# The first rows of a fused convolution in another order, and its products in 64 slots instead of 72

## The chip, the cores and the metric

One core of one Trainium2 chip runs the whole program. The metric is the device time of one execution in microseconds (us), and lower is better.

## The reference, cut to what matters

Two layers are computed on x (8, 256, 512). The change lies in the first block alone, a gated causal convolution ("long convolution" with 32 filters, heads of 8 channels). In it k and v are both the context and q is the normalised x:

```python
k_ = k.reshape(B, H, head_dim, L)
...
kv = jnp.einsum('bhil,bhjl->bijhl', k_, v_)
...
y = jnp.fft.irfft(kv_f * kernel_f, n=fft_size)[..., :L]
out = y + kv * D[None, None, None, :, None]
out = jnp.einsum('bijhl,bhil->bjhl', out, q_)
...
x = x + jnp.tanh(g_xattn[0]) * _L0_xattn_ref(ctx_2048, ctx_2048, _layernorm(x, axis=-1), L0_xattn_ssm_kernel, L0_xattn_D, 8)
```

Here B is 8, H is 32, head_dim is 8 and L is 512. As k equals v, only 36 of the 64 products (i, j) of a head differ. All three later blocks (a mixture of experts, linear attention, soft mixture of experts) start from this block's output and are the same in both kernels.

## The kernel before

`conv_stage` is one block in which every engine has a program written out by hand. Only semaphores join them. What stands in an engine's program behind an instruction that waits, waits too.

**Rows.** The context rows (`c`) and the x rows (`q`) are turned by TensorE in units of 8 transposes of 128x128: `("c", 0, 0..3)` and `("q", 0, 0..3)` for the first half of the heads, `("c", 1, ..)` and `("q", 1, ..)` for the second. A unit fills one of three banks of the PSUM tensor `ring`. ScalarE (`put`) and, for the units named in `by_dve`, VectorE for one half of it, copy it to `c_e` or `q_e`. Before x rows are turned, VectorE takes their statistics (`normalise`), ScalarE the root (`ln.root`), and VectorE writes the normalised rows (`scale`). There are four such norms, of 4 row blocks each.

**Steps.** There are 16 steps of two heads. In step s VectorE makes the products of the context with itself for step s+2 (`pairs`, into `prod`), ScalarE rounds them to float16 (`split`, `prod_hi`), and GpSimd subtracts to get the rest (`prod_lo`, L299). TensorE multiplies both with Toeplitz tiles `toep`, read from a DRAM copy `ssm_split` of the filters that the kernel itself stores at the start: `convolve(s, m)` for m = 0 to 3, with 6(m+1) matmuls of 288 columns, 60 in a step. VectorE multiplies the result with q (`weigh(s, m)`, L429 to L431) into the slots of `terms`, 16 columns each. TensorE sums the slots by accumulating transposes (`add_up`, L524), 9 of them for 72 slots, 8 of which hold zeros from a memset. VectorE adds the residual (`add_rows`, L440). TensorE's order is `convolve(s, m)` and then the sum of two positions earlier; a `ring` bank is reused after three units and `terms` has three buffers. The turns of the second half stand between the positions of steps 1 to 4.

**Queues.** The SP queue loads rows and residuals and stores results. The ACT queue stores `ssm_split` and loads every `toep`. Behind that, GpSimd and ScalarE split the experts' down weights in 24 parts (`load_part`, `rest_of_parts`, `split_parts`), which the next stage needs. ScalarE's program in step s is: load `toep` for step s+1, its puts, `split(s + 2)`, `split_parts(s)`.

Of the kernel before, what the change touches and what calls it, by code (L numbers as in the profile page):

```python
# [14 lines left out]
ACT = mybir.ActivationFunctionType  # L15
ALU = mybir.AluOpType
# [3 lines left out]
B, N, D = 8, 256, 512  # L20
# [100 lines left out]
PAIRED = 2 * B * PAIRS  # L121
SLOTS_T = 9
RUN = 8 * SLOTS_T
WRAP = SSM_I + 4
# [17 lines left out]
def conv_stage(nc, k, x, ctx, ssm_reversed, ssm_d, g_xattn, g_ffn, ssm_split, x1, down, down_whole, down_tail):  # L142
# [5 lines left out]
    with phase(nc) as st:  # L148
# [16 lines left out]

        ident_zeroed, ident_ready, gates_loaded, gates_ready, zeroed = (
            sem(n) for n in ("ident_zeroed", "ident_ready", "gates_loaded", "gates_ready", "zeroed"))
        ssm_loaded, d_added, ssm_hi, ssm_lo, ssm_stored = (sem(n) for n in ("ssm_loaded", "d_added", "ssm_hi", "ssm_lo", "ssm_stored"))
# [25 lines left out]
        units = [(t, 0, n) for t in "cq" for n in range(4)]  # L194
        later = {1: ("c", 0), 2: ("c", 2), 3: ("q", 0), 4: ("q", 2)}
        for s in range(STEPS):
# [5 lines left out]
        turns = {unit: n for n, unit in enumerate(u for u in units if u[0] != "conv")}  # L202
        by_dve = {unit: n for n, unit in enumerate(u for u in units if u[0] == "c" and not u[1])}

# [33 lines left out]
        @block.sync  # L238
        def _(sp):
            def load(t, g, u):  # L240
                for e in range(2):
                    src = (c_t if t == "c" else x_t)[g, e, :, u * 4:u * 4 + 4, :]
                    sp.dma_start(rows[t][e * 64:e * 64 + 64, u * 4:u * 4 + 4, :], src).then_inc(loaded[t][u], 16)

            def load_res(s):
                if s >= 2:
                    sp.wait_ge(added, s - 1)
                sp.dma_start(res[:, s % 2, :], rows_at(x, s)).then_inc(res_loaded[s % 2], 16)

            def store(s):  # L250
                sp.wait_ge(added, s + 1)
                sp.dma_start(rows_at(x1, s), gated[:, s % 2, :]).then_inc(stored[s % 2], 16)

            for t in "cq":
                for u in range(2):
                    load(t, 0, u)
            load_res(0)
            load_res(1)
            for u in range(2):
                sp.wait_ge(turned["c"], 2 * u + 2)  # L260
                load("c", 1, u)
            for u in range(2):
                sp.wait_ge(normed, 4 * u + 4)
                load("q", 1, u)
            for s in range(STEPS):
                store(s)
                if s + 2 < STEPS:
                    load_res(s + 2)
            for u in range(2):
                sp.wait_ge(stored[u], STEPS // 2 * 16)  # L270

        @block.gpsimd
        def _(pool):
# [3 lines left out]
                                    base=0, pattern=[[-1, P]], channel_multiplier=1).then_inc(ident_ready, 1)  # L277
            nc.gpsimd.memset(terms[:, :, :, :], 0.0).then_inc(zeroed, 1)

# [14 lines left out]
            for s in range(STEPS):  # L294
                u = s % 2
                pool.wait_ge(hi_done, s + 1)
                if s >= 2:
                    pool.wait_ge(conv_done, (s - 1) * KD)
                nc.gpsimd.tensor_tensor(prod_lo[:, u].rearrange("p k e r -> p (k e r)"), prod[:, u, :],  # L299
                                        prod_hi[:, u].rearrange("p k e r -> p (k e r)"), ALU.subtract).then_inc(lo_done, 1)  # L300
                if s == 0:
                    for n in range(PART_BUFS):
                        load_part(n)
                if s >= 2:
                    rest_of_parts(s - 2)
# [6 lines left out]
        def _(act):  # L312
# [3 lines left out]
            act.dma_start(k.gates[:, 2:4], g_ffn.partition_broadcast(P)).then_inc(gates_loaded, 16)  # L316
            act.wait_ge(gates_loaded, 32)
            nc.scalar.activation(k.tanh_gates[:, :], k.gates[:, :], ACT.Tanh).then_inc(gates_ready, 1)
            act.wait_ge(d_added, 1)
            nc.scalar.activation(ssm_q[:, 0, :], ssm[:, :], ACT.Copy).then_inc(ssm_hi, 1)  # L320
            nc.scalar.preload_act_table(ACT.Sqrt)
            act.wait_ge(ssm_lo, 1)
            act.dma_start(ssm_split.rearrange("s e q d -> e s (q d)"), ssm_q[:, :, :].rearrange("h q d -> h (q d)")).then_inc(ssm_stored, 16)
            act.wait_ge(ssm_stored, 16)
            for s in range(T_BUFS):
                toeplitz(act, s)

# [22 lines left out]

            for n in range(4):
                put(("c", 0, n))
            split(0)
            for n in range(2):
                ln.root(nc, act, n)
                put(("q", 0, 2 * n))
                put(("q", 0, 2 * n + 1))
            split(1)
            for s in range(STEPS):
                if s >= 1 and s - 1 + T_BUFS < STEPS:  # L360
                    act.wait_ge(conv_done, s * KD)
                    toeplitz(act, s - 1 + T_BUFS)
                if s in (2, 3):
                    ln.root(nc, act, s)
                if s in later:
                    t, first = later[s]
                    put((t, 1, first))
                    put((t, 1, first + 1))
                if s + 2 < STEPS:
                    split(s + 2)  # L370
                split_parts(s)

        @block.vector
        def _(dve):
# [4 lines left out]

            for n in range(4):  # L380
                dve.wait_ge(turned["c"], n + 1)
                for dst, src in turned_in(("c", 0, n), 1):
                    last = nc.vector.tensor_copy(dst, src)
                last.then_inc(out_dve, 1)

            def pairs(s):
# [18 lines left out]
            def weigh(s, m):  # L405
# [5 lines left out]
                if n == 0:  # L411
                    dve.wait_ge(out_act, turns["q", 0, 3] + 1)
                    dve.wait_ge(zeroed, 1)
                if s == GSTEPS and m == 0:
# [15 lines left out]
                nc.vector.tensor_tensor(to(40, (8 * 2 * B, 3), (2, 64)), values(8, (64, 3), (1, 64)), weights(1, (B, 3), (1, 64)), ALU.mult)  # L430
                last = nc.vector.tensor_tensor(to(64, (4 * 2 * B, 2), (2, 32)), values(32, (0, 2), (1, 32)), weights(4, (32, 2), (1, 32)), ALU.mult)  # L431
                last.then_inc(weighed, 1)
# [28 lines left out]
            pairs(0)  # L461
            for n in range(2):
                normalise(n)
                scale(n)
            pairs(1)
            dve.wait_ge(gates_ready, 1)
            for s in range(STEPS):
                weigh(s, 0)
                if s in (2, 3):
                    normalise(s)  # L470
                weigh(s, 1)
                if s in (2, 3):
                    scale(s)
                weigh(s, 2)
# [1949 lines left out]
```

## Time and profile before

| | us |
|---|---|
| median of 3 runs | 1817.76 |
| lowest, highest | 1815.56, 1821.31 |
| the profiled execution | 1817.87 |
| its span in the profile | 1816.1 |

The profiled execution is 0.11 above the median; 1.8 us of it lie outside the span. All times below are from the span's start. Of the page, TensorE is busy 87% of the span, VectorE 60%, ScalarE 42%, GpSimd 29%. The convolution ends with its last `add_rows` at 264.48; the next stage begins to load after the last store, and everything after it depends on that store.

A row of a timeline gives start, duration, engine, line and operation, tiles written and read, shapes and count; in brackets is the idle time before it and what ended that. A row with a count spans several instructions. A row of windows gives for a stretch the busy time and count of each engine, then TensorE's granted clock (1.00 is 2.4 GHz, 0.50 is 1.2 GHz), the busy share of the DMA engines and their rate.

### The profile page before, as it was taken

How to read it: one execution, taken by the hardware profiler on the slowest of the kernel's cores; microseconds unless marked ns; L12 is line 12 of the kernel's file. 1: busy time of each engine (PE TensorE's matmuls, PEld its weight loads, DVE VectorE, ACT ScalarE, POOL GpSimd, SP SyncE). 2: the span in 40 equal slices, each digit the busy share in tenths (PEclk: the TensorE clock that was granted, in tenths of full speed). 3: DMA queues.
4: the chain of work that ended last, by engine and by line, in shares of the span. 5: the costliest groups of instructions: out<-in, count | busy, mean ns of one | idle time of the engine just before them, and what ended most of it. 6: DMA issues, size and time to landing. Idle time of an engine off the chain costs nothing. (4 is left out here: it accounts for less than half of the span.)

```text
span 1816.1 us, 27604 instructions
## 1 busy us (share of the span) xinstructions
PE 1583.9 (87%) x9596; PEld 925.9 (51%) x9596; DVE 1083.5 (60%) x2154; ACT 754.6 (42%) x1390; POOL 519.0 (29%) x428
## 2 busy tenths in 40 slices
PE   2879985999979999777898984979999999999997
PEld 1668872444446666434453542445555555555554
DVE  4778854543632223277676857566767767675664
ACT  2543213333412233144343431465565646565462
POOL 2347850434422344333434332101102020101101
PEclk6889997999989999978999997989999999999999
DMA  9435545433475665353515124651432505142341
GB/s 191 96 92 144 160 137 178 134 110 111 153 208 147 175 180 150 121 199 116 159 63 162 59 93 149 260 108 42 88 68 60 110 23 121 23 104 52 65 85 44
DMA packets 274042, 215.18 MB, mean 118 GB/s; under 512 B 184514, under 2 KB 222914, under 8 KB 272274
## 3 DMA queue, kind: packets, MB, share of 16 engines
q1 hardware_dynamic: 232640, 152.53, 31.9%
q10 hardware_dynamic: 32034, 31.10, 5.9%
q0 software_dynamic: 9264, 30.15, 5.5%
q8 instruction: 66, 1.08, 0.2%
q14 instruction: 38, 0.31, 0.1%
HBM read 120.33 MB, written 49.63 MB: 94 GB/s over the span
## 5 line engine op out<-in xcount | busy, mean ns | idle before, releaser
L2018 POOL TENSOR_TENSOR s_h_lo<-s_h,s_h_hi 128x512 f16<-128x512 f32 x32 | 36.9, 1154 | 554.2 <-DVE s_h_hi L2229 554.2
L1205 DVE TENSOR_TENSOR e_h<-e_up,e_silu 128x352 f32<-128x352 f32 x39 | 20.5, 525 | 149.8 <-ACT e_silu L1164 146.5
L511 PE MATMUL ring<-prod_hi,toep 128*128 128x288 f16 x320 | 94.7, 296 | 13.5 <-DVE terms L431 12.9
L299 POOL TENSOR_TENSOR prod_lo<-prod,prod_hi 128x2304 f16<-128x2304 f32 x16 | 73.3, 4584 | 107.2 <-ACT prod_hi L341 107.2
L2247 PE MATMUL s_ring<-w_mu,s_xt_hi 128*128 128x512 f16 x256 | 98.7, 386 | 4.2 <-DVE s_xt_lo L2150 3.9
L2249 PE MATMUL s_ring<-w_mu,s_xt_lo 128*128 128x512 f16 x256 | 98.5, 385 | 0.0
L2248 PE MATMUL s_ring<-w_mu,s_xt_hi 128*128 128x512 f16 x256 | 98.4, 384 | 0.0
L2247 PE MATMUL s_acc<-w_w,s_g_hi 128*128 128x512 f16 x256 | 97.1, 379 | 0.1
L2247 PE MATMUL s_ring<-w_w,s_xt_hi 128*128 128x512 f16 x256 | 97.0, 379 | 0.0
L2248 PE MATMUL s_ring<-w_w,s_xt_hi 128*128 128x512 f16 x256 | 97.0, 379 | 0.0
L2249 PE MATMUL s_ring<-w_w,s_xt_lo 128*128 128x512 f16 x256 | 97.0, 379 | 0.0
L2249 PE MATMUL s_acc<-w_w,s_g_lo 128*128 128x512 f16 x256 | 97.0, 379 | 0.0
L2248 PE MATMUL s_acc<-w_w,s_g_hi 128*128 128x512 f16 x256 | 97.0, 379 | 0.0
L2155 DVE TENSOR_REDUCE s_top<-s_lg 128x1 f32<-128x512 f32 x64 | 43.9, 686 | 88.6 <-ACT s_lg L2061 88.4
L513 PE MATMUL ring<-prod_hi,toep 128*128 128x288 f16 x320 | 94.5, 295 | 0.0
L512 PE MATMUL ring<-prod_lo,toep 128*128 128x288 f16 x320 | 94.5, 295 | 0.0
L1164 ACT ACTIVATE e_silu<-e_gate 128x352 f32<-128x352 f32 x39 | 18.1, 463 | 174.8 <-PE e_up L1107 174.8
L2067 ACT ACTIVATE s_dt<-s_ring,s_slot_low 128x256 f32<-128x256 f32 x128 | 59.4, 469 | 52.4 <-DVE s_dq L2177 52.2
L2232 DVE TENSOR_TENSOR s_g_lo<-s_ring,s_g_hi 128x512 f16<-128x512 f32 x64 | 43.6, 690 | 58.7 <-ACT s_g_hi L2098 58.7
L524 PE MATMUL rows_total<-ident,terms 128*128 128x128 f32 x576 | 73.7, 274 | 0.0
L1083 POOL DMA_INDIRECT e_rows<-normed_rows,slot_token x39 | 37.4, 958 | 124.8 <-DMA e_xt<-e_rows 122.8
L781 POOL TENSOR_TENSOR h_lo<-silu_h,h_hi 128x512 f16<-128x512 f32 (+1 forms) x24 | 30.8, 1283 | 146.5 <-ACT h_hi L746 146.5
(376 smaller groups left out, 4771.0 us busy)
## 6 DMA issues: line engine op xcount, KB each, us to landing
expert_rows<-e_y SPq DMA_DIRECT2D x39, 256.0 KB
toep<-ssm_split ACTq DMA_DIRECT2D x16, 512.0 KB
a_part_in<-in_L_ffn_W ACTq DMA_DIRECT2D x32, 256.0 KB
w_split<-a_part_q ACTq DMA_DIRECT2D x32, 256.0 KB, 2.5
w_w<-w_split SPq DMA_DIRECT2D x8, 1024.0 KB, 15.5
stage<-in_L_ffn_gate_w SPq DMA_DIRECT2D x8, 704.0 KB
stage<-in_L_ffn_up_w SPq DMA_DIRECT2D x8, 704.0 KB
c_rows<-in_ctx SPq DMA_DIRECT2D x8, 512.0 KB
```

The costliest lines, as they stand in the source:

```text
L299: nc.gpsimd.tensor_tensor(prod_lo[:, u].rearrange("p k e r -> p (k e r)"), prod[:, u, :], prod_hi[:, u].rearrange("p k e r -> p (k e r)"), ...
L511: nc.tensor.matmul(out, w_hi, hi, start=(n == 0), stop=False)
L512: nc.tensor.matmul(out, w_hi, lo, start=False, stop=False)
L513: last = nc.tensor.matmul(out, w_lo, hi, start=False, stop=(n == m))
L524: last = nc.tensor.matmul(out, terms[:, n % M_BUFS, o * 8:o * 8 + 8].rearrange("p j n -> p (j n)"), k.ident[:, :], is_transpose=True, star ...
L1083: nc.gpsimd.indirect_dma_start(rows[:, n % U, :], None, xn, bass.IndirectOffsetOnAxis(ap=k.slot_token[:, n:n + 1], axis=0)).then_inc(gathe ...
L2067: last_ = A(dt[:, n % 2, e, :], ring[:, bank, e * N:(e + 1) * N], ACT.Exp, bias=slot_low[:, n % 4, e:e + 1], accum_out=slot_sum[:, 2 * n + ...
L2155: V.tensor_reduce(top[:, t, j:j + 1], lg[:, t, j * D:(j + 1) * D], AX.X, ALU.max).then_inc(S["top_done"], 1)
L2232: V.tensor_tensor(g[1][:, n % G_BUFS, :], ring[:, bank, :], g[0][:, n % G_BUFS, :], ALU.subtract).then_inc(S["g_lo"], 1)
L2247: mm(out_, a[0], b_[0], start=first, stop=False)
L2248: mm(out_, a[0], b_[1], start=False, stop=False)
L2249: return mm(out_, a[1], b_[0], start=False, stop=last_)
```

## The change

- **Slots.** The products of a position go to 64 slots, all of which are written: four multiplies by VectorE (512, 384, 64 and 64 elements) instead of three (512, 384, 128), 8 transposes in a sum instead of 9. The memset of `terms` and its semaphore are gone.
- **Filters.** ScalarE rounds the filters first. The tanh of the gates, with the table load that follows, stands behind the first two context puts. The first two `toep` loads move from ACT's queue to SP's, behind the x rows and a wait for `ssm_stored`, ahead of the residuals and the second half's context rows.
- **First kernel half.** `prod_lo` of step 0 is made by VectorE between statistics and scaling of the first norm, not by GpSimd. The loads of the first three weight parts move with GpSimd's program from step 0 to step 1.
- **x rows.** VectorE copies one half of units `("q", 0, 2)` and `("q", 0, 3)`. The root of norm 1 stands behind the put of the first x unit.
- **Second half.** The x rows are turned in steps 4 and 6 instead of 3 and 4. Norm 2 has its statistics in step 2 and its scaling in step 3, norm 3 in steps 4 and 5; before, each had both in one step, 2 and 3.

```diff
-SLOTS_T = 9
+SLOTS_T = 8
...
-        later = {1: ("c", 0), 2: ("c", 2), 3: ("q", 0), 4: ("q", 2)}
+        later = {1: ("c", 0), 2: ("c", 2), 4: ("q", 0), 6: ("q", 2)}
...
-        by_dve = {unit: n for n, unit in enumerate(u for u in units if u[0] == "c" and not u[1])}
+        by_dve = {unit: n for n, unit in enumerate(u for u in units if u[0] != "conv" and not u[1] and (u[0] == "c" or u[2] >= 2))}
...
+            sp.wait_ge(ssm_stored, 16)
+            for s in range(T_BUFS):
+                toeplitz(sp, s)
             load_res(0)
...
-                if s == 0:
+                if s == 1:
                     for n in range(PART_BUFS):
                         load_part(n)
...
-            act.wait_ge(ssm_stored, 16)
-            for s in range(T_BUFS):
-                toeplitz(act, s)
...
             for n in range(4):
+                if n == 2:
+                    act.wait_ge(gates_loaded, 32)
+                    nc.scalar.activation(k.tanh_gates[:, :], k.gates[:, :], ACT.Tanh).then_inc(gates_ready, 1)
+                    nc.scalar.preload_act_table(ACT.Sqrt)
                 put(("c", 0, n))
             split(0)
-            for n in range(2):
-                ln.root(nc, act, n)
-                put(("q", 0, 2 * n))
-                put(("q", 0, 2 * n + 1))
+            ln.root(nc, act, 0)
+            for n in range(4):
+                put(("q", 0, n))
+                if n == 0:
+                    ln.root(nc, act, 1)
...
-                last = nc.vector.tensor_tensor(to(64, (4 * 2 * B, 2), (2, 32)), values(32, (0, 2), (1, 32)), weights(4, (32, 2), (1, 32)), ALU.mult)
+                nc.vector.tensor_tensor(to(8, (9 * 2 * B, 4), (2, B)), values(32, (B, 4), (1, B)), weights(4, (B, 4), (1, B)), ALU.mult)
+                last = nc.vector.tensor_tensor(to(36, (2, 32)), values(32, (1, 32)), weights(0, (1, 32)), ALU.mult)
...
-                if s in (2, 3):
-                    normalise(s)
+                if s in (3, 5):
+                    scale((s + 1) // 2)
                 weigh(s, 1)
-                if s in (2, 3):
-                    scale(s)
+                if s in (2, 4):
+                    normalise(1 + s // 2)
```

ScalarE at the start, before: tanh, the filters, their store and the two Toeplitz loads stand ahead of the first put (`c_e<-ring`).

```order
L318 ACT_TABLE_LOAD
L318 ACTIVATE tanh_gates<-gates 128x4
L320 ACTIVATE ssm_q<-ssm 32x640
L321 ACT_TABLE_LOAD
L323 DMA ssm_split<-ssm_q 2x16x1280
L236 DMA toep<-ssm_split 128x4x512 x2
L333 ACTIVATE c_e<-ring 128x64x8
```

The same place after:

```order
L322 ACT_TABLE_LOAD
L322 ACTIVATE ssm_q<-ssm 32x640
L324 DMA ssm_split<-ssm_q 2x16x1280
L331 ACTIVATE c_e<-ring 128x64x8
L331 ACTIVATE c_e<-ring 128x64x4
L331 ACTIVATE c_e<-ring 128x64x8
L331 ACTIVATE c_e<-ring 128x64x4
L352 ACTIVATE tanh_gates<-gates 128x4
L353 ACT_TABLE_LOAD
```

The Toeplitz loads have left this queue, and tanh and the table of the root stand behind two puts.

VectorE around the first norm, after against before (`L84` to `L105` are statistics and variance, `L109` and the `xq` rows the scaling):

```order
 L102 TENSOR_SCALAR x_spread<-x_spread 128x4
 L105 TENSOR_TENSOR x_var<-x_gap,x_spread 128x4
+L471 TENSOR_TENSOR prod_lo<-prod,prod_hi 128x2304
 L109 RECIPROCAL x_rstd<-x_std 128x4
-L458 TENSOR_SCALAR xq<-x_rows,x_mean,x_rstd 128x512 x4
+L465 TENSOR_SCALAR xq<-x_rows,x_mean,x_rstd 128x512 x4
```

The rest of the kernel's first products is now one VectorE instruction ahead of the scaling.

VectorE in step 3, after, between the first two positions (`weigh`, four rows each):

```order
L438 TENSOR_TENSOR terms<-ring,q_e 128x2x32
L109 RECIPROCAL x_rstd<-x_std 128x4
L465 TENSOR_SCALAR xq<-x_rows,x_mean,x_rstd 128x512 x4
L435 TENSOR_TENSOR terms<-ring,q_e 128x2x4x64
L436 TENSOR_TENSOR terms<-ring,q_e 128x2x192
L437 TENSOR_TENSOR terms<-ring,q_e 128x2x4x8
L438 TENSOR_TENSOR terms<-ring,q_e 128x2x32
```

Before, the scaling of the same norm stood in step 2, one position behind its own statistics.

## Rows read from the trace of the kernel before

**Rows 1.** Windows of the convolution's stretches: from, to, length, busy times, clock.

```profile
54.60:91.30 36.70, 33.30 (x271) 27.83 (x269) 29.73 (x49) 20.12 (x25) 18.15 (x9) 0.96 0.32 81
91.30:128.90 37.60, 27.45 (x180) 21.43 (x178) 28.12 (x48) 15.41 (x20) 12.52 (x9) 0.82 0.35 95
...
158.02:169.30 11.28, 11.28 (x98) 9.85 (x97) 9.39 (x16) 2.65 (x2) 10.69 (x8) 1.00 0.60 176
169.30:180.58 11.28, 11.28 (x98) 9.85 (x97) 10.14 (x17) 3.17 (x3) 7.82 (x6) 1.00 0.45 139
```

**Rows 2.** Timeline of ScalarE and its queue, start.

```profile
11.07 0.20 ACT L318 ACTIVATE tanh_gates<-gates 128x4 f32<-128x4 f32 x1 [6.73 <-DMA gates<-in_g_ffn]
...
11.92 1.28 ACT L321 ACT_TABLE_LOAD   x1
12.78 1.48 ACTq L323 DMA_DIRECT2D ssm_split<-ssm_q  x1
23.58 0.96 ACTq L236 DMA_DIRECT2D toep<-ssm_split  x2
24.59 5.72 ACT L333 ACTIVATE c_e<-ring 128x512 f32<-128x512 f32 x8 [11.39 <-issue]
33.00 2.12 ACT L341 ACTIVATE prod_hi<-prod 128x2304 f16<-128x2304 f32 x1 [2.69 <-DVE prod L403]
```

**Rows 3.** Timeline of TensorE, start.

```profile
9.19 3.65 PE L496 MATMUL ring<-ident,c_rows 128*128 128x128 f32 x16 [9.19 <-DMA c_rows<-in_ctx]
...
54.64 0.45 PE L511 MATMUL ring<-prod_hi,toep 128*128 128x288 f16 x1
```

**Rows 4.** Timeline of VectorE, from the first products to the first weighing.

```profile
30.34 2.29 DVE L402 TENSOR_TENSOR prod<-c_e 128x2048 f32<-128x2048 f32 x1 [0.60 <-ACT c_e L333]
...
32.88 2.47 DVE L84 BATCH_NORM_STATS2 x_stats<-x_rows 128x6 f32<-128x512 f32 x4
35.38 4.38 DVE L95 TENSOR_TENSOR x_mean<-x_stats 128x4 f32<-128x4 f32 x1
...
59.12 0.69 DVE L429 TENSOR_TENSOR terms<-ring,q_e 128x512 f32<-128x512 f32 x1 [4.62 <-ACT q_e L333]
...
60.19 0.28 DVE L431 TENSOR_TENSOR terms<-ring,q_e 128x128 f32<-128x128 f32 x1
60.39 0.68 DVE L429 TENSOR_TENSOR terms<-ring,q_e 128x512 f32<-128x512 f32 x1
```

**Rows 5.** Timeline of GpSimd, start.

```profile
35.21 4.54 POOL L299 TENSOR_TENSOR prod_lo<-prod,prod_hi 128x2304 f16<-128x2304 f32 x1 [30.74 <-ACT prod_hi L341]
39.69 1.92 POOL L282 DMA_DIRECT2D part_in<-in_L_ffn_down_w  x3
```

**Rows 6.** Waits of TensorE from 54.5 to 265.5: in total, times, longest.

```profile
PE ring L511 <- DVE terms L431: 12.9, 5, 3.6
```

**Rows 7.** Timeline of TensorE in step 1: a sum, then the next position.

```profile
73.42 1.15 PE L524 MATMUL rows_total<-ident,terms 128*128 128x128 f32 x9
74.40 0.29 PE L511 MATMUL ring<-prod_hi,toep 128*128 128x288 f16 x1
```

**Rows 8.** Timeline of VectorE, the norms of steps 2 and 3, the end.

```profile
84.59 4.41 DVE L105 TENSOR_TENSOR x_var<-x_gap,x_spread 128x4 f32<-128x4 f32 x1
...
102.97 3.65 DVE L95 TENSOR_TENSOR x_mean<-x_stats 128x4 f32<-128x4 f32 x1
...
117.41 1.91 DVE L458 TENSOR_SCALAR xq<-x_rows,x_mean,x_rstd 128x512 f32<-128x512 f32 x4 [7.78 <-PE ring L496]
...
264.48 0.75 DVE L440 SCALAR_TENSOR_TENSOR gated<-rows_total,tanh_gates,res 128x512 f32<-128x512 f32 x1 [1.59 <-PE rows_total L524]
```

**Rows 9.** Windows by ten microseconds; the last columns are DMA share and GB/s.

```profile
10.00:20.00 10.00, 3.94 (x22) 3.30 (x20) 5.05 (x7) 2.12 (x3) 0.00 (x0) 0.81 1.07 216
20.00:30.00 10.00, 1.97 (x8) 1.57 (x8) 1.54 (x2) 5.41 (x8) 0.00 (x0) 0.50 1.08 181
...
50.00:60.00 10.00, 8.14 (x43) 6.30 (x44) 5.35 (x9) 6.82 (x9) 0.00 (x0) 0.64 0.72 140
```

**Rows 10.** DMA issues up to 60 us: count, size of one, time to landing.

```profile
toep<-ssm_split ACTq DMA_DIRECT2D x2, 512.0 KB
...
part_in<-in_L_ffn_down_w POOLq DMA_DIRECT2D x2, 256.0 KB, 7.7
```

More of the change, by code:

```diff
@@ L164, in conv_stage @@
         ring, total = ps("ring", [P, RING, 2, D]), ps("rows_total", [P, 2, D])
-        ident_zeroed, ident_ready, gates_loaded, gates_ready, zeroed = (
-            sem(n) for n in ("ident_zeroed", "ident_ready", "gates_loaded", "gates_ready", "zeroed"))
+        ident_zeroed, ident_ready, gates_loaded, gates_ready = (
+            sem(n) for n in ("ident_zeroed", "ident_ready", "gates_loaded", "gates_ready"))
         ssm_loaded, d_added, ssm_hi, ssm_lo, ssm_stored = (sem(n) for n in ("ssm_loaded", "d_added", "ssm_hi", "ssm_lo", "ssm_stored"))
@@ L277, in _ @@
                                     base=0, pattern=[[-1, P]], channel_multiplier=1).then_inc(ident_ready, 1)
-            nc.gpsimd.memset(terms[:, :, :, :], 0.0).then_inc(zeroed, 1)
             def load_part(n):
@@ L295, in _ @@
                 u = s % 2
-                pool.wait_ge(hi_done, s + 1)
+                if s:
+                    pool.wait_ge(hi_done, s + 1)
                 if s >= 2:
                     pool.wait_ge(conv_done, (s - 1) * KD)
-                nc.gpsimd.tensor_tensor(prod_lo[:, u].rearrange("p k e r -> p (k e r)"), prod[:, u, :],
-                                        prod_hi[:, u].rearrange("p k e r -> p (k e r)"), ALU.subtract).then_inc(lo_done, 1)
-                if s == 0:
+                if s:
+                    nc.gpsimd.tensor_tensor(prod_lo[:, u].rearrange("p k e r -> p (k e r)"), prod[:, u, :],
+                                            prod_hi[:, u].rearrange("p k e r -> p (k e r)"), ALU.subtract).then_inc(lo_done, 1)
+                if s == 1:
                     for n in range(PART_BUFS):
@@ L316, in _ @@
             act.dma_start(k.gates[:, 2:4], g_ffn.partition_broadcast(P)).then_inc(gates_loaded, 16)
-            act.wait_ge(gates_loaded, 32)
-            nc.scalar.activation(k.tanh_gates[:, :], k.gates[:, :], ACT.Tanh).then_inc(gates_ready, 1)
             act.wait_ge(d_added, 1)
             nc.scalar.activation(ssm_q[:, 0, :], ssm[:, :], ACT.Copy).then_inc(ssm_hi, 1)
-            nc.scalar.preload_act_table(ACT.Sqrt)
             act.wait_ge(ssm_lo, 1)
             act.dma_start(ssm_split.rearrange("s e q d -> e s (q d)"), ssm_q[:, :, :].rearrange("h q d -> h (q d)")).then_inc(ssm_stored, 16)
-            act.wait_ge(ssm_stored, 16)
-            for s in range(T_BUFS):
-                toeplitz(act, s)
             def put(unit):
@@ L362, in _ @@
                     toeplitz(act, s - 1 + T_BUFS)
-                if s in (2, 3):
-                    ln.root(nc, act, s)
                 if s in later:
@@ L368, in _ @@
                     put((t, 1, first + 1))
+                if s in (2, 4):
+                    ln.root(nc, act, 1 + s // 2)
                 if s + 2 < STEPS:
@@ L378, in _, with put_half @@
             nc.vector.tensor_tensor(ssm_q[:, 1, :], ssm[:, :], ssm_q[:, 0, :], ALU.subtract).then_inc(ssm_lo, 1)
-            for n in range(4):
-                dve.wait_ge(turned["c"], n + 1)
-                for dst, src in turned_in(("c", 0, n), 1):
+            def put_half(t, n):
+                dve.wait_ge(turned[t], n + 1)
+                for dst, src in turned_in((t, 0, n), 1):
                     last = nc.vector.tensor_copy(dst, src)
                 last.then_inc(out_dve, 1)
+            for n in range(4):
+                put_half("c", n)
             def pairs(s):
@@ L412, in weigh @@
                     dve.wait_ge(out_act, turns["q", 0, 3] + 1)
-                    dve.wait_ge(zeroed, 1)
+                    dve.wait_ge(out_dve, len(by_dve))
                 if s == GSTEPS and m == 0:
@@ L461, in _ @@
             pairs(0)
-            for n in range(2):
-                normalise(n)
-                scale(n)
+            normalise(0)
+            dve.wait_ge(hi_done, 1)
+            nc.vector.tensor_tensor(prod_lo[:, 0].rearrange("p k e r -> p (k e r)"), prod[:, 0, :],
+                                    prod_hi[:, 0].rearrange("p k e r -> p (k e r)"), ALU.subtract).then_inc(lo_done, 1)
+            scale(0)
+            normalise(1)
+            scale(1)
             pairs(1)
+            for n in (2, 3):
+                put_half("q", n)
             dve.wait_ge(gates_ready, 1)
@@ L468, in _ @@
                 weigh(s, 0)
-                if s in (2, 3):
-                    normalise(s)
+                if s in (3, 5):
+                    scale((s + 1) // 2)
                 weigh(s, 1)
-                if s in (2, 3):
-                    scale(s)
+                if s in (2, 4):
+                    normalise(1 + s // 2)
                 weigh(s, 2)
```

## The prediction

> **What bounds the kernel now.** I read the timelines of the start first, then windows over the stretches of the convolution, then TensorE's waits. Only the stage up to the last `add_rows` at 264.48 [rows 8] changes; what follows waits for its last store, so a microsecond won there should be one won at the end. The stage falls into three parts. Up to 54.64, when the first convolution matmul starts [rows 3], TensorE does little: engines wait in turn for one another. From 54.6 to 128.9, in 74.3 us, it is busy 33.30 + 27.45 = 60.75, and its clock is 0.96 and 0.82 of full [rows 1]. In the steady part it is busy 11.28 of 11.28 us in a step, with VectorE at 9.39 to 10.14 [rows 1]: TensorE bounds there, and VectorE is not far behind.
>
> **The start, step by step.** Before, ScalarE waits to 11.07 for the gates, and to 23.58 for the store of `ssm_split` issued at 12.78, since the two Toeplitz loads stand ahead of its puts; the first put starts at 24.59, though the first rows were turned from 9.19 on [rows 2, 3]. After, nothing of this stands ahead of the puts. I lay the new order out with the old durations:
> - The 16 transposes at 9.19 take 3.65, so unit c0 is there at 11.1 and c1 at 12.9 [rows 3]. A put with one half on each engine costs ScalarE 5.72/4 = 1.43 [rows 2]. Puts c0 and c1 end at 14.3; tanh and a table load add 0.20 + 1.28 [rows 2], to 15.8; c2 and c3 end at 18.7.
> - `pairs(0)` starts at 18.8, not 30.34, and takes 32.88 - 30.34 = 2.54 [rows 4]: 21.3. Statistics 2.47, to 23.8; the seven small instructions take 0.9 where nothing holds them, to 24.7. Before, the first of them took 4.38, beside GpSimd's `prod_lo` of 4.54 [rows 4, 5]. That instruction is now VectorE's. Its price is not in the trace: 2048 elements took 2.29 [rows 4], 2304 at that pace are 2.6, and GpSimd's 4.54 is the far end; I take 2.5 to 2.6, as it is the same kind of work on the same engine: 27.3. Its input `prod_hi` (2.12 [rows 2]) is ready at 23.6 and holds nothing.
> - Scaling costs 0.2 + 1.91 [rows 8]; two of four row blocks are there at 28.5, all at 29.5. TensorE turns q0 and q1 from 28.5 to 32.2 (3.65 [rows 3]). ScalarE puts both halves of q0, twice 1.43, from 30.4 to 33.3, then takes the root of norm 1. VectorE has done that norm's statistics by 32.8, scales from 33.6 to 35.8, and TensorE turns q2 and q3 from 34.8 to **38.5**. There the first convolution matmul can start, against 54.64: **16.1 us earlier**.
> - VectorE makes `pairs(1)` to 38.4 and its two halves of q2 and q3 to 41.3; the first weighing is at 41.4, against 59.12 [rows 4], so VectorE gains 17.7 and does not hold TensorE more than before.
>
> The cover for the first Toeplitz loads: they go behind 4 MB of rows, which at 216 GB/s [rows 9] drain at about 22 to 24, and behind `ssm_stored`, at 18.6 if the store keeps its 10.8 us from issue [rows 2] and is issued at 7.8. Two loads of 512 KB [rows 10] at 181 GB/s [rows 9] take 5.8: landed near 30 to 32, 6 to 8 us before use. Residuals and second context rows go behind them, to about 45; these are used past 50. If that cover is gone, each microsecond costs one.
>
> **The slots.** A sum of 9 transposes takes 74.40 - 73.42 = 0.98, so one is 0.109 [rows 7]. There are 64 sums: 64 x 0.109 = **7.0 us** off TensorE, all of it on the path where TensorE bounds. A step becomes 11.28 - 0.44 = 10.84. VectorE pays: the 128-element multiply took 60.39 - 60.19 = 0.20 and the two longer ones 60.19 - 59.12 = 1.07 for 896 elements [rows 4], so an instruction costs 0.066 plus 1.05 ns an element. Two of 64 elements cost 0.27 instead of 0.20: +0.07 a position, +0.27 a step. The far end is a full 0.20 each, +0.8 a step. With 9.39 to 10.14 in a step now [rows 1] VectorE reaches 9.7 to 10.4 of 10.84, so I count this at nothing; at the far end it is 10.2 to 10.9, which no longer hides.
>
> These two short multiplies read PSUM. The Trainium skill, page "VectorE: DVE Perf Modes", section "The TRN2 errata — SBUF-src ops pay a fixed extra latency per instruction", gives a fixed 120 cycles for a PSUM source; an estimate from it is 0.19 for a short multiply, nearly the far end, +0.7 a step. The rows put the fixed part at 0.066, so I stay with them.
>
> **Steps 1 to 6.** From 54.64 to 265.23, the end of the last `add_rows` [rows 8], are 210.6 us. TensorE's work in it is 16 steps of 11.28 and 8 units of turns of 0.87 (8 transposes of 0.109): 187.4. The remaining 23.2 are waits for `terms`, 12.9 in 5 [rows 6], about 3 of tail behind the last matmul, and some 7 of half clock, at the start and behind the waits (0.82 [rows 1]). Why the waits: in steps 2 and 3 VectorE carries a whole norm of about 5.5 beside its 9.4 to 10.1, one small instruction stood 4.41 and another 3.65 beside GpSimd, and the last scaling waited 7.78 for a turn that TensorE had queued behind convolution work [rows 8]. After, steps 2 and 4 carry 3.3 and steps 3 and 5 carry 2.1, and the scaling of norm 3 in step 5 finds its turns done in step 4: the 7.78 goes. What is late next is the statistics in steps 2 and 4: 9.7 to 10.4 + 3.3 is 13.0 to 13.7, plus up to 4.4 beside GpSimd, against 10.84 + 1.74 = 12.6 for TensorE. That is 0.4 to 5.5 of shortage in each of two steps, some of it taken up by the three buffers. I take for after the same 3 of tail, 1.5 of half clock at the start, and 5 of waits with 3 of half clock behind them, 12.4 instead of 23.2: **10.8 us** won; ends are 0 (the waits merely move) and 16 (hardly any is left).
>
> **Sum.** 16.1 + 7.0 + 10.8 = 33.9. The profiled execution of 1817.87 becomes 1784.0. It stands 0.11 above the median, so I take it for the median.
>
> **Rivals.**
> 1. **A transfer takes part of it.** The first weight parts are now issued after GpSimd's `prod_lo(1)`, at about 47, not 39.69 [rows 5]. With 7.7 to land [rows 10] they arrive at 54, and ScalarE waits for the first in `split_parts(0)`; queued behind it are the Toeplitz load of step 2 and the put of the next turn. Step 2 wants that load at about 61.5. About 10 MB must move by then, and DMA was busy to the fifties before too [rows 9]. The `ssm_split` store, on the same queue beside a full SP queue, took 10.8 us [rows 2]: then the load lands at 65, TensorE waits 4 and loses 2 of clock, and a second one of that size may follow: 1790, to 1796. The Trainium skill, page "DMA: Bandwidth & Descriptors", section "Queues, rings and completion order", says that each DMA engine goes round-robin between the queues' rings; by that rule the load would not stand behind SP's rows, would land near 60, and the sum would stay 1784. The store's row speaks against leaning on it.
> 2. **The first Toeplitz tiles are late.** Nobody waited for them before, so the trace bounds their landing only by 54.64, 31 us from issue at 23.58 [rows 2, 3]. With the same from 22 the start would gain 1.6, not 16.1: 1798. The DMA rates speak for 30.
> 3. **VectorE becomes the bound in the steady steps**, because its second input and GpSimd meet more often at a shorter step, or the short multiplies cost 0.20. Its step is then 11.2 instead of 10.84, in 16 steps 5.8: 1790.
> 4. **Slower than before**: the same mechanism with a high price. VectorE's step without the two short ones is 9.39 to 10.14 less 4 x 0.20, about 9. To undo 26.9 of other gains and add 0.3%, a step must last (26.9 + 5.5)/16 = 2.0 more than 11.28, 13.3; that takes 8 short multiplies of 0.54 each. Decided from there on; at 0.6 the time would be 1831. No row of an instruction so short is near it.
> 5. **The second half's waits vanish**: all 16 us are won: 1779.
>
> That the change does not do what it says can be left aside: the order shows 8 transposes and the moved norms.
>
> **How the numbers follow.** Likeliest, 1784 with its own range of 1779 to 1790: 0.55. Rival 1: 0.17. Rival 2, in whole or part: 0.07. Rival 3: 0.09. Rival 5 and a little beyond: 0.09. Rival 4: 0.02; an unnamed loss, 0.01. The range from 1775 to 1798 takes in rivals 1, 3 and 5. About 0.3%, 5.5 us, is what a measurement of this kernel can tell from no change: faster 0.96, within it 0.02, slower 0.02.
>
> **What would show it.** First put of ScalarE near 11, first products near 19, first convolution matmul near 38.5 with no wait on `toep`, first weighing near 41.5; steady steps 10.84 apart with TensorE busy throughout; short multiplies at 0.13 from start to start; the last `add_rows` near 231. A wait of TensorE ahead of step 2's first matmul, with ScalarE idle ahead of the first `part_q`, is rival 1. A VectorE with no idle time in the steady steps is rival 3. The forecast is wrong if the stage ends past 245, or if a later stage gives time back.

## The result and the profile after

Before: 1817.11 us (median of 4 runs, 1815.56 to 1821.31). After: 1786.62 us (median of 4, 1785.37 to 1789.42). The ratio is 0.9831, 95% interval 0.9812 to 0.9851: **faster by 1.7%**, 2.6 us above the forecast of 1784.0 and inside its range. The profiled execution took 1787.78, its span 1786.1. The forecast was worked out from one profiled execution, and profile against profile the gain is 30.1 where 33.9 were forecast.

The convolution stage ends at 234.82 + 0.75 = 235.57, against 265.23: 29.7 us earlier, where 33.9 were forecast. What follows takes 1786.1 - 235.6 = 1550.5, and took 1816.1 - 265.2 = 1550.9, so the whole gain reaches the end. In the profiles of the experiments below this rest varied between 1546.5 and 1554.1 with nothing in it changed. So **stage ends**, read from the profile, compare kernels more closely than total times do, and stand beside them. They carry the chance of the start, which varied between 37.7 and 38.4 among kernels that start alike. The length of the convolution alone repeats better: 197.28 in the changed kernel, 197.19 and 197.16 in two kernels below (e2, e3) that differ from it only ahead of the first matmul.

ScalarE and its queue at the start, timeline after (columns as in [rows 2]):

```profile
8.16 1.22 ACTq L324 DMA_DIRECT2D ssm_split<-ssm_q  x1
10.91 3.27 ACT L331 ACTIVATE c_e<-ring 128x512 f32<-128x512 f32 x4 [3.62 <-PE ring L509]
13.96 0.22 ACT L352 ACTIVATE tanh_gates<-gates 128x4 f32<-128x4 f32 x1
```

The first put starts at 10.91, not 24.59 [rows 2]. SP and VectorE, after, from the Toeplitz loads to the first weighing:

```profile
18.64 0.98 SPq L236 DMA_DIRECT2D toep<-ssm_split  x2
...
18.98 2.29 DVE L408 TENSOR_TENSOR prod<-c_e 128x2048 f32<-128x2048 f32 x1
...
24.80 2.55 DVE L471 TENSOR_TENSOR prod_lo<-prod,prod_hi 128x2304 f16<-128x2304 f32 x1
27.27 0.17 DVE L109 RECIPROCAL x_rstd<-x_std 128x4 f32<-128x4 f32 x1
27.48 1.92 DVE L465 TENSOR_SCALAR xq<-x_rows,x_mean,x_rstd 128x512 f32<-128x512 f32 x4
...
41.29 0.69 DVE L435 TENSOR_TENSOR terms<-ring,q_e 128x512 f32<-128x512 f32 x1
```

TensorE, after: the first convolution matmul, then the sum and the turn ahead of step 2 and its first matmul.

```profile
38.29 0.29 PE L524 MATMUL ring<-prod_hi,toep 128*128 128x288 f16 x1
...
59.10 1.04 PE L537 MATMUL rows_total<-ident,terms 128*128 128x128 f32 x8
59.97 1.04 PE L509 MATMUL ring<-ident,c_rows 128*128 128x128 f32 x8
60.85 0.29 PE L524 MATMUL ring<-prod_hi,toep 128*128 128x288 f16 x1
```

It starts at 38.29, and step 2 at 60.85 without idle time. TensorE's waits from 38.2 to 235.6, after (in total, times, longest), then windows (columns as in [rows 1]):

```profile
PE rows_total L537 <- DVE terms L438: 6.2, 7, 1.7
PE ring L524 <- DVE terms L438: 4.7, 2, 2.9
PE ring L524 <- DVE q_e L386: 0.7, 1, 0.7
```

```profile
54.60:91.30 36.70, 33.73 (x273) 29.06 (x272) 34.39 (x60) 18.01 (x23) 20.12 (x15) 0.95 0.47 128
91.30:128.90 37.60, 31.83 (x266) 26.94 (x265) 35.84 (x74) 17.85 (x21) 22.30 (x13) 1.00 0.46 122
...
38.29:73.58 35.29, 34.58 (x294) 29.82 (x291) 31.39 (x66) 18.18 (x21) 20.59 (x13) 1.00 0.66 150
150.54:161.38 10.84, 10.84 (x94) 9.41 (x92) 9.54 (x21) 2.65 (x2) 10.25 (x8) 1.00 0.57 175
38.29:235.57 197.28, 184.72 (x1538) 158.03 (x1535) 175.22 (x337) 69.52 (x76) 134.93 (x87) 0.99 0.53 147
```

Two things are unlike the forecast. TensorE waits 11.6 in all, not 5. And VectorE is busy 34.39 and 35.84 of some 37 us, where it was 29.73 and 28.12 [rows 1] (the record of an instruction includes the time for which it is held up): it has become the engine that sets the pace in steps 2 to 6. Its timeline there, and under it GpSimd's:

```profile
67.96 2.70 DVE L95 TENSOR_TENSOR x_mean<-x_stats 128x4 f32<-128x4 f32 x1
...
79.74 6.56 DVE L465 TENSOR_SCALAR xq<-x_rows,x_mean,x_rstd 128x512 f32<-128x512 f32 x4
...
108.08 7.01 DVE L465 TENSOR_SCALAR xq<-x_rows,x_mean,x_rstd 128x512 f32<-128x512 f32 x4
```

```profile
66.05 4.57 POOL L303 TENSOR_TENSOR prod_lo<-prod,prod_hi 128x2304 f16<-128x2304 f32 x1 [7.42 <-ACT prod_hi L339]
...
79.20 4.55 POOL L303 TENSOR_TENSOR prod_lo<-prod,prod_hi 128x2304 f16<-128x2304 f32 x1 [3.28 <-ACT prod_hi L339]
83.71 1.34 POOL L290 TENSOR_TENSOR part_q<-part_in,part_q 128x512 f16<-128x512 f32 x1
...
108.34 4.72 POOL L303 TENSOR_TENSOR prod_lo<-prod,prod_hi 128x2304 f16<-128x2304 f32 x1 [4.06 <-ACT prod_hi L339]
113.02 1.34 POOL L290 TENSOR_TENSOR part_q<-part_in,part_q 128x512 f16<-128x512 f32 x1
```

Four scalings that take 1.92 alone took 6.56 and 7.01; the first of the four alone took 4.30 of the 6.56. Each time GpSimd had a `prod_lo` running, and then its subtraction for the weight parts (`part_q`). In the steady steps `pairs` meets GpSimd in the same way. Groups of VectorE from 130 to 235, after (busy, mean ns of one, idle before):

```profile
L408 DVE TENSOR_TENSOR prod<-c_e 128x2048 f32<-128x2048 f32 x8 | 26.7, 3340 | 0.0
...
L409 DVE TENSOR_TENSOR prod<-c_e 128x256 f32<-128x256 f32 x8 | 8.1, 1016 | 0.0
```

A `pairs`, the sum of these two means, costs 4.36 there and 2.71 at the start (2.29 and 0.42). The steps last mostly 10.85 and 11.55 in turn: 89.9 us for the eight from 139.83 to 229.72, where 8 x 10.84 is 86.7.

### The profile page after: what moved, and what is told of

Read it like the earlier page. It is cut to its first block and busy times, and to the rows that moved or that the text cites. A ratio compares the mean times of both kernels' runs of the same rounds, so it can differ in the third digit from the quotient of the medians.

```text
span 1786.1 us, 27541 instructions
## 1 busy us (share of the span) xinstructions
PE 1571.0 (88%) x9532; PEld 915.7 (51%) x9532; DVE 1094.1 (61%) x2223; ACT 752.3 (42%) x1386; POOL 513.2 (29%) x426
## 5 line engine op out<-in xcount | busy, mean ns | idle before, releaser
L524 PE MATMUL ring<-prod_hi,toep 128*128 128x288 f16 x320 | 92.2, 288 | 5.6 <-DVE terms L438 4.7
L303 POOL TENSOR_TENSOR prod_lo<-prod,prod_hi 128x2304 f16<-128x2304 f32 x15 | 69.1, 4607 | 86.8 <-ACT prod_hi L339 86.8
L526 PE MATMUL ring<-prod_hi,toep 128*128 128x288 f16 x320 | 92.1, 288 | 0.0
L339 ACT ACTIVATE prod_hi<-prod 128x2304 f16<-128x2304 f32 x16 | 34.1, 2128 | 92.9 <-DVE prod L409 85.7
## 6 DMA issues: line engine op xcount, KB each, us to landing
w_w<-w_split SPq DMA_DIRECT2D x8, 1024.0 KB, 16.1
```

The costliest lines, as they stand in the source:

```text
L524: nc.tensor.matmul(out, w_hi, hi, start=(n == 0), stop=False)
L526: last = nc.tensor.matmul(out, w_lo, hi, start=False, stop=(n == m))
```

## The experiments

**Theory.** The missing 4 us are VectorE waiting for GpSimd: a VectorE instruction that reads two operands from SBUF, and a scaling too, cannot run beside a GpSimd instruction (the port theory). **Rivals.** VectorE simply has too much to do with the fourth multiply (the load theory); or the parts of the change are worth other amounts than I gave them. Unless said otherwise each kernel is the changed one with one edit, and its stage end stands against 235.57. In brackets behind each time are its ratio to the kernel before, run beside it, and the 95% interval of that ratio.

### One part undone

Nine transposes and three multiplies again:

```diff
-SLOTS_T = 8
+SLOTS_T = 9
```

> The changed kernel with 72 slots again: three multiplies, 9 transposes a sum, the memset back; all the rest as changed. Theory A (the sum as predicted): TensorE bounds, so the slots are worth their full 7.0 us, the stage ends at about 242.6 and the time is about 1794. Theory B (part of the 7.0 is given back, because VectorE now arrives late in every other steady step): before, steps of 11.28 had TensorE busy throughout; changed, they are 10.85 and 11.55 in turn, 11.2 on average. Then steady steps of 11.28 return without waits ahead of a sum, the stage ends at 237 to 240 and the time is 1789 to 1791.

Measured: 1788.44 (0.9845, 0.9823 to 0.9867), convolution from 37.83 to 236.49: 198.7 us long against 197.3. The steady steps last exactly 11.28 with no wait, and the waits sum to 8.1:

```profile
PE rows_total L538 <- DVE terms L439: 4.1, 4, 1.3
PE ring L525 <- DVE terms L439: 4.0, 2, 2.6
```

So here the slots are worth **1.4 us, not 7.0**. Two things take up the rest. In the changed kernel TensorE is idle for 3.7 us more (197.28 - 184.72 against 198.66 - 189.77), mostly in waits for VectorE. And its busy time is only 5.05 shorter instead of 7.0; among other things its granted clock from 78.4 to 85.0, behind the longest wait, was 0.74 there and 1.00 in this kernel. That is the direction of the theory in which something else sets the pace, and more strongly than it foresaw.

ScalarE's start as before (tanh, table and both Toeplitz loads ahead of the puts):

```diff
-            sp.wait_ge(ssm_stored, 16)
-            for s in range(T_BUFS):
-                toeplitz(sp, s)
...
+            act.wait_ge(ssm_stored, 16)
+            for s in range(T_BUFS):
+                toeplitz(act, s)
```

> The changed kernel with ScalarE's start as before: tanh, its table load, the filter store, the wait for it and the two Toeplitz loads stand ahead of the first put again, and SP no longer issues those two. If the queue order at the start is what made the first half of the gain, the first put is at 24 to 25 instead of 10.9, the first convolution matmul comes 9 to 13 us later than 38.3, and the time is 1796 to 1800. If a transfer would have held the start anyway (rival), the loss is under 4 us.

Measured: 1798.97 (0.9908, 0.9884 to 0.9932); convolution from 50.17, stage end 247.36, 11.8 later. Of the 16.35 us won at the start, 11.9 are this part's. The first put (24.97), the first matmul and the time all fell where the first expectation had put them.

The first `prod_lo` on GpSimd again:

```diff
-                if s:
-                    pool.wait_ge(hi_done, s + 1)
+                pool.wait_ge(hi_done, s + 1)
```

> The changed kernel with the first prod_lo on GpSimd again (weight parts still load in step 1). If two instructions of VectorE with both inputs in SBUF wait for GpSimd's whole 4.54 us, the small ones behind the statistics or the scaling wait for it: first turn of x rows about 1.5 to 2.5 us later than 28.6, and so the first convolution matmul at 40 to 41; time +1 to +3 us. If VectorE's own 2.5 us are the same as the wait, no difference.

Measured: 1789.52 (0.9849, 0.9826 to 0.9872); convolution from 40.60, end 237.76: 2.3 and 2.2 later. VectorE, timeline of this kernel:

```profile
24.17 4.38 DVE L95 TENSOR_TENSOR x_mean<-x_stats 128x4 f32<-128x4 f32 x1
```

An instruction on 128x4 values, 0.17 alone, waits for the whole `prod_lo` again, as in [rows 4]. VectorE does the subtraction itself in 2.55 and still comes out ahead.

Norms and turns of the second half where they were:

```diff
-        later = {1: ("c", 0), 2: ("c", 2), 4: ("q", 0), 6: ("q", 2)}
+        later = {1: ("c", 0), 2: ("c", 2), 3: ("q", 0), 4: ("q", 2)}
...
-                if s in (3, 5):
-                    scale((s + 1) // 2)
+                if s in (2, 3):
+                    normalise(s)
```

> The changed kernel with the second half's norms and turns as before: statistics and scaling both in steps 2 and 3, x rows turned in steps 3 and 4. The prediction gave 10.8 us to the waits of steps 1 to 6, the trace shows some 6. If the new places are the cause, the 7.8 us wait of the last scaling for a turn returns, TensorE's waits for terms up to step 6 are 11 to 15 instead of 7.6, and the time is 1792 to 1797. If the earlier start alone did it, under 2 us are lost.

Measured: 1797.59 (0.9901, 0.9880 to 0.9922), stage end 246.22, from 37.94: 208.3 us long against 197.3. TensorE's waits are 18.0, and the last scaling waits 7.70 for its turn, as in [rows 8]. The time is 0.6 above the range expected. The moved norms are worth **11.0**, where 10.8 were forecast. Start 16.35, slots 1.4 and norms 11.0 make 28.8 of the 29.7 won, so the three parts nearly add up, and taken this way the whole shortage lies with the slots. The kernel before gives a rough second reading: with the norms in their old places the slots bring 210.6 - 208.3 = 2.3, and with nine transposes the norms bring 210.6 - 198.7 = 11.9.

### GpSimd's work taken away

GpSimd's subtraction for the weight parts does 16 of 512 columns (the rest of those low halves is left out):

```diff
-part_q[0:rows_, v, 1, :], part_in[0:rows_, v, :], part_q[0:rows_, v, 0, :]
+part_q[0:rows_, v, 1, 0:16], part_in[0:rows_, v, 0:16], part_q[0:rows_, v, 0, 0:16]
```

> The changed kernel with GpSimd's subtraction for the weight parts cut to 16 of 512 columns (the low halves of the experts' down weights are left out; their buffer is filled with zeros once). It takes about a quarter of GpSimd's work away and leaves prod_lo. Port theory (VectorE's instructions with both inputs in SBUF, and the scalings, wait until GpSimd's instruction ends): pairs get shorter on average by 0.3 to 0.8 us, the waits of TensorE in the steady steps fall by half or more, the stage ends 1 to 3 us earlier. Load theory (VectorE simply has too much work with the fourth multiply): no change of the stage's end beyond 0.5 us.

Measured: 1777.92 (0.9794, 0.9766 to 0.9821), end 228.66, 6.9 earlier, every steady step 10.84 or 10.85. VectorE's `pairs` in this kernel, 130 to 235:

```profile
L411 DVE TENSOR_TENSOR prod<-c_e 128x2048 f32<-128x2048 f32 x7 | 17.3, 2466 | 0.0
```

VectorE's own program is untouched, its four multiplies included. This refutes the load theory. The port theory had the direction right and the size wrong, since 1 to 3 us were expected. The trace of the changed kernel shows why parts this short cost so much. VectorE, then GpSimd:

```profile
162.70 4.51 DVE L408 TENSOR_TENSOR prod<-c_e 128x2048 f32<-128x2048 f32 x1
```

```profile
159.26 4.69 POOL L303 TENSOR_TENSOR prod_lo<-prod,prod_hi 128x2304 f16<-128x2304 f32 x1
163.79 1.27 POOL L290 TENSOR_TENSOR part_q<-part_in,part_q 128x512 f16<-128x512 f32 x1
```

`pairs` waits through the rest of `prod_lo` and then through the subtraction behind it as well: it ends at 167.21, 2.15 after the latter. This happens in every other steady step, and those are the long ones.

GpSimd's `prod_lo` of steps 1 to 15 does 16 of 2304 columns (the low halves of the products are left out):

```diff
-                                            prod_hi[:, u].rearrange("p k e r -> p (k e r)"), ALU.subtract)
+                                            prod_hi[:, u].rearrange("p k e r -> p (k e r)")[:, 0:16], ALU.subtract)
```

> The changed kernel with GpSimd's prod_lo of steps 1 to 15 cut to 16 of 2304 columns (the low half of the products is left out there, the buffer holds zeros). Port theory: both scalings fall from 6.56 and 7.01 to about 2, pairs to 2.3, all steady steps are 10.84 and TensorE waits for terms less than 3 us in the whole stage; the stage ends 5 to 8 us earlier, near 228 to 231. Load theory: scalings shorten, but the steady steps stay 11.2 on average.

Measured: 1774.08 (0.9770, 0.9743 to 0.9797), end 222.35, 13.2 earlier, where 5 to 8 were expected. The scalings take 1.92 and 1.91 and the long instruction of `pairs` 2.28; TensorE waits 1.2. These 13.2 us are not the price of `prod_lo` alone: with it gone, GpSimd's subtractions no longer fall beside `pairs` either. They are what GpSimd's work as a whole, where it stands, costs this stage.

`prod_lo` in three instructions of 768 columns:

```diff
+                    for i in range(3):
+                        last = nc.gpsimd.tensor_tensor(lo_[:, i * W:i * W + W], prod[:, u, i * W:i * W + W], hi_[:, i * W:i * W + W], ALU.subtract)
```

> The changed kernel with GpSimd's prod_lo in three pieces of 768 columns; nothing is left out. If the one that waits gets its turn at the end of GpSimd's current instruction, a scaling waits at most 1.6 us instead of 4.3 each time, and the stage ends 1 to 4 us earlier. If GpSimd's next piece goes first, nothing changes; more instructions of GpSimd cost at most 0.2 us a step, which is hidden.

Measured: 1789.27 (0.9853, 0.9826 to 0.9880), end 238.03, **2.5 worse**. VectorE, then GpSimd, of this kernel:

```profile
80.61 6.27 DVE L468 TENSOR_SCALAR xq<-x_rows,x_mean,x_rstd 128x512 f32<-128x512 f32 x4
```

```profile
80.08 5.22 POOL L306 TENSOR_TENSOR prod_lo<-prod,prod_hi 128x768 f16<-128x768 f32 x3 [3.28 <-ACT prod_hi L342]
```

The four scalings took 1.38 to 1.87 each: no long wait for one, but each waits for a piece. Here the engines take turns, one instruction for one, so shorter pieces hardly shorten the sum for four instructions in a row. The 2.5 are lost elsewhere, and neither expectation had them: in the steady part the long steps rise from some 11.55 to some 12.07, as a `pairs` there waits for the last piece and the subtraction behind it and takes 5.04 (at 163.58) where it took 4.51.

### The waits moved out of the way

ScalarE scales norms 2 and 3; VectorE makes only the offset `x_shift`, 128x4:

```diff
+                    for t in range(4):
+                        nc.scalar.activation(blocks(xn[:, t, :]), flipped(half[:, t, :]), ACT.Identity,
+                                             bias=shift[:, t:t + 1], scale=ln.rstd[:, t:t + 1]).then_inc(normed, 1)
```

> The changed kernel with norms 2 and 3 scaled by ScalarE (x times 1/std plus a shift that VectorE prepares), nothing left out. VectorE loses two scalings of 6.56 and 7.01 us. If they make TensorE's waits behind them (2.9 in step 3, 1.8 to 4.8 in step 5), the stage ends 3 to 6 us earlier and the time is 1781 to 1784. If the waits come from elsewhere, under 1 us. ScalarE gets 2 x 3 us more, beside 70% idle.

Measured: 1780.34 (0.9801, 0.9774 to 0.9829), end 230.89, 4.7 earlier, the steady steps as they were.

In addition, the variance of norms 2 and 3 one position later:

```diff
-                ln.variance(nc, dve, n)
+                if not late:
+                    ln.variance(nc, dve, n)
...
+                if s in (2, 4):
+                    ln.variance(nc, dve, 1 + s // 2)
```

> The kernel with norms 2 and 3 scaled by ScalarE, and in steps 2 and 4 the seven small instructions of the variance moved behind the third weighing; the statistics stay where they are, nothing is left out. Changed, the first small one waited 2.7 us beside GpSimd's prod_lo, and TensorE waited 2.9 us in step 3 behind it. Port theory: the small ones find GpSimd idle, that wait falls under 1 us, the stage ends 2 to 4 us earlier than the 230.9 with ScalarE's scaling alone, time 1776 to 1779. If it is VectorE's amount of work, the wait stays.

Measured: 1781.61 (0.9815, 0.9787 to 0.9844), end 230.37: 0.5 more, where 2 to 4 were expected. A miss. VectorE of this kernel, GpSimd's `prod_lo` starting at 79.13:

```profile
72.85 3.71 DVE L417 TENSOR_TENSOR prod<-c_e 128x2048 f32<-128x2048 f32 x1
...
79.67 4.03 DVE L495 SCALAR_TENSOR_TENSOR x_shift<-x_mean,x_rstd 128x4 f32<-128x4 f32 x1
```

The waits only moved on to the next two-operand instructions: `pairs` took 3.71 instead of 2.28, beside a subtraction for the parts, and the tiny `x_shift` 4.03. Moving VectorE's work by one place does not help while GpSimd's keeps its place.

So GpSimd's order was changed alone, in the changed kernel: the subtraction of the parts right behind VectorE's `pairs`, while ScalarE still rounds, and their stores behind `prod_lo`; ScalarE splits its parts ahead of the products:

```diff
+                if s > 2:
+                    pool.wait_ge(prod_done, s + 1)
+                    low_parts(s - 2)
```

> The changed kernel with only that order of GpSimd's parts. Port theory: the steady steps become 10.84 each, 3 to 4 us off the stage's end of 235.6, while the scalings of steps 3 and 5 still wait for GpSimd 4 to 6.5 us; time 1783 to 1785.

Measured: 1781.62 (0.9809, 0.9780 to 0.9838), end 230.75, 4.8 earlier; all steady steps 10.84, the scalings still 5.81 and more. That is slightly better than expected. It cures the steady part and not steps 3 and 5.

ScalarE's scaling (e8), the late variance (e9) and the new order of GpSimd (e11) together:

> As e9, and from step 3 on GpSimd subtracts the weight parts as soon as VectorE's products of a step are done, while ScalarE still rounds them, and not behind its prod_lo; it issues their stores and loads after prod_lo. ScalarE rounds its parts ahead of the products. Nothing is left out. Port theory: the parts no longer meet the next products, steady steps become 10.84 each as with the parts cut short, 3 to 4 us less than e9: stage end 224 to 226, time 1771 to 1775. If the part loads come too late in this order, ScalarE waits for them and TensorE for prod_lo, and it is slower than e9.

Measured: **1773.43** (1772.57 to 1776.86; 0.9775, 0.9751 to 0.9800), convolution from 37.72 to 222.87. It leaves nothing out, and its stage ends 12.7 us before that of the changed kernel. VectorE's `pairs` (130 to 235), the whole convolution as a window, and TensorE's waits in it:

```profile
L430 DVE TENSOR_TENSOR prod<-c_e 128x2048 f32<-128x2048 f32 x7 | 17.9, 2554 | 0.0
```

```profile
37.72:222.87 185.15, 182.24 (x1537) 157.70 (x1535) 150.90 (x330) 75.59 (x84) 124.72 (x87) 0.99 0.60 157
```

```profile
PE ring L551 <- DVE terms L460: 1.9, 1, 1.9
```

TensorE is busy 182.2 of 185.2 us, and VectorE has shed 24.3 (175.22 to 150.90), 13.6 of them the two scalings that ScalarE now does. Nearly all of the 13.2 us that e6 won by leaving work out is won here with all of the work done, by order and by handing over the scalings.

The same kernel with nine transposes again:

```diff
-SLOTS_T = 8
+SLOTS_T = 9
```

> The kernel with the second weighing and part of the norms free of GpSimd (parts subtracted first, ScalarE scaling in steps 2 and 3), now with 72 slots and nine transposes a sum again. Put against 222.87 us of the same kernel with 64 slots, and 1773.4 us of time.
> Theory A, the waits behind GpSimd are what hid the slots' worth (0.9 us where they were put back in the changed kernel): with those waits gone, each of 64 sums costs TensorE its 0.109 us more and nothing takes it up: steps of 11.28 in place of 10.84, the convolution stage ends 6.2 to 7.0 us later, at 229 to 230, time near 1780.
> Theory B, the slots are worth little in any order, since VectorE's chain of sums takes the time either way: end at 223 to 225, time 1774 to 1775, and steps that stay below 11.1.

Measured: 1784.41 (0.9826, 0.9796 to 0.9855), convolution from 38.10 to 228.87, steady steps 11.28, one wait of 1.3. The end is 6.0 later, of which 0.4 is the start: the slots are worth **5.6**, against 1.4 in the changed kernel. The theory that the waits hid them holds; the expected 6.2 to 7.0 was slightly high, since the wait is 0.6 shorter here and takes up that much.

## Why the prediction was right, and where it was off

- **The start: right, nearly to the microsecond.** Forecast 16.1 won and a first matmul at 38.5; measured 16.35 and 38.29. Put 10.91 (11.1), first products 18.98 (18.8), first scaling 27.48 (27.3), weighing 41.29 (41.4). The one price with two far ends, VectorE's `prod_lo`, took 2.55, inside the 2.5 to 2.6 worked out from the 2048-element row. The clock was better than assumed: I gave 1.5 us to half clock at the start, and the granted clock of 38.29 to 73.58 is 1.00. That was luck: it was 0.50 from 21.1 to 38.2, and in e10, whose start is the same, it was still 0.50 from 37.72 to 39.60.
- **Not taken apart**: of the 16.35, ScalarE's order brings 11.9 (e2) and VectorE's `prod_lo` 2.3 (e3); the other 2.1 belong to the remaining edits of the start.
- **The slots: the arithmetic right, the place wrong.** A sum of eight transposes takes 0.109 less, and a step without waits is 10.84 (the window of 150.54). The two short multiplies stand at 0.13 from start to start, as forecast (in a position of the steady part they start at 146.14 and 146.27, the next instruction at 146.40). The step that failed is "all of it on the path where TensorE bounds": in the changed kernel the saving ran into VectorE's waits, and putting the ninth transpose back cost 1.4 (e1), not 7.0.
- **Steps 1 to 6: the mis-sized term.** I took 12.4 us beside TensorE's work of 180.4 (16 x 10.84 and 8 x 0.87 are 180.4, plus 12.4 is 192.8) and got 197.28 - 180.4 = 16.9. The waits are 11.6 instead of 5; clock and tail are 5.3 instead of 7.5. This is the same shortage as the slots', booked elsewhere: undone by itself, the move of the norms is worth its 10.8 (e4), and it is the slots' saving that comes back, mostly as waits. The waits were too small because the working let only the statistics meet GpSimd ("plus up to 4.4 beside GpSimd") and gave steps 3 and 5 their 2.1 as they were. In [rows 8] the scaling at 1.91 was one that happened to meet nothing. The other one, in the trace of before, had stood at 3.19, and I did not ask why:

```profile
90.39 3.19 DVE L458 TENSOR_SCALAR xq<-x_rows,x_mean,x_rstd 128x512 f32<-128x512 f32 x4
```

  The scalings took 6.56 and 7.01, 9.7 us more than 3.84, and handing both to ScalarE brought 4.7 (e8).
- **Rival 3, given 0.09, came half true.** The steady step became 11.24 on average, not 11.2 in all 16: of 8 steps about 3.2 us. Its first reason (the second input meets GpSimd more often at a shorter step) is what e5 and e11 show; its second, short multiplies of 0.20, is not: they last 0.21 but the next starts 0.13 after. From the 120 cycles for a PSUM source in the Trainium skill, page "VectorE: DVE Perf Modes", section "The TRN2 errata — SBUF-src ops pay a fixed extra latency per instruction", the prediction had an estimate of 0.19. That is near the 0.21 of one record, but a row of such multiplies costs 0.13 each, and the measurement decides.
- **Rival 1, a transfer in the way: its first half happened, its end did not.** ScalarE waited 3.47 for the first weight part, and the load for step 2 was issued only at 54.76. But step 2 wanted it at 60.85, 6.1 later, and did not wait. The load landed in 4.3, at 59.1 (the row below), where 10.8 was the bound from the store.
- **Rival 2, late first tiles**: issued at 18.64, they landed in 7.0, and nobody waited. Rivals 4 and 5 did not happen; e10 is the kernel that rival 5 imagined, and its time of 1773.4 goes beyond that rival's 1779.
- **Nothing was given back** by a later stage, as assumed.

DMA issues of the changed kernel up to 60 us (count, size, time to landing):

```profile
toep<-ssm_split SPq DMA_DIRECT2D x2, 512.0 KB, 7.0
...
toep<-ssm_split ACTq DMA_DIRECT2D x1, 512.0 KB, 4.3
```

What stays open: which of the edits in e10 carries the last part. The 4.7 of e8 and the 4.8 of e11 make 9.5 of its 12.7; the other 3.2 may be the late variance, worth 0.5 while GpSimd kept its order, or the way they meet; no run parts the two. Open too is what decides which engine goes next when both wait.

## What to carry to other kernels

Work out a shorter step for every engine with the rows *beside* its neighbours, not with the shortest row: an instruction's price on VectorE was 0.17 or 4.4, depending on whether GpSimd was running. Before a saving on the bound engine is counted in full, ask whether the next engine can follow; here the same edit was worth 1.4 and, with the other engine's waits gone, 5.6. And where two engines exclude each other, move the one with slack into the other's gap (between `pairs` and the end of the rounding), rather than shift the victim by a place.

## What the runs showed of the hardware

- **A scaling waits as well.** `TENSOR_SCALAR` from SBUF to SBUF on 128x512 took 4.30 beside a `prod_lo` on GpSimd, about 0.5 alone. I had reckoned with this only for instructions that read two tensors from SBUF. The Trainium skill says so, page "SBUF — State Buffer", section "Who interferes with whom": `tensor_scalar` can enter a mode that uses both ports, and whoever issues first holds the shared pair for the whole instruction. The scaling rows agree (`prod_lo` from 79.20, the scaling from 79.74), and I had not weighed that sentence. The order of the recorded starts does not settle every case, though: the `pairs` at 162.70 let the subtraction that starts at 163.79 go first.
- **Size does not matter to the wait**: 128x4 values took 4.03 (e9) and 4.38 (e3), 0.16 alone. VectorE's multiplies with one operand in PSUM ran at their usual 0.68 beside a `prod_lo` (the changed kernel, 147.72, with `prod_lo` from 147.39 to 151.97).
- **It holds in both directions.** GpSimd's part subtraction, which takes 1.15 to 1.34 in most places, took 3.21 while VectorE's `pairs` ran. GpSimd, then VectorE, of the changed kernel:

```profile
141.65 3.21 POOL L290 TENSOR_TENSOR part_q<-part_in,part_q 128x512 f16<-128x512 f32 x1
```

```profile
140.49 3.36 DVE L408 TENSOR_TENSOR prod<-c_e 128x2048 f32<-128x2048 f32 x1
143.77 1.38 DVE L409 TENSOR_TENSOR prod<-c_e 128x256 f32<-128x256 f32 x1
```

- **They often alternate, but not always.** With `prod_lo` in three pieces the four scalings took 1.38 to 1.87 each (e7): each waited for one instruction of GpSimd, not for the burst, and a row of short ones paid once each. In the steady steps `pairs` went ahead of the subtraction at 141.65, but at 162.70 it waited for two GpSimd instructions in a row.
